# First batch of a four-stage residual kernel: w2 sent by ScalarE and subj_w by SyncE, every tile of x added on TensorE, the adapter's first product in two column tiles with the odd tiles' relu on VectorE, empty matmuls fed from a 128x128 tile

## What is computed

```python
    x = x + _L0_cond_ref(x, itok_B_0_8, L0_cond_W1, L0_cond_b1, L0_cond_W2, L0_cond_b2, L0_cond_gamma, L0_cond_beta)
    x = x + _L1_cond_ref(x, itok_B_0_7, L1_cond_weight, L1_cond_bias)
    x = x + _L2_cond_ref(x, itok_B_0_2, L2_cond_expert_wi, ...)
    x = x + _L3_cond_ref(x, L3_cond_W1, L3_cond_b1, L3_cond_v, itok_B_0_2)
```

## Time and profile before

| | us |
|---|---|
| median of 3 runs | 497.57 (497.13 to 498.37) |
| the profiled execution's own time | 497.3 |
| its span (first to last instruction) | 495.5 |
| PE busy in the span | 488.9 |

### The profile page before, as it was taken

One profiled execution on the slowest core, in us unless ns is written; L12 is line 12 of the kernel. 1 busy time (PEld: TensorE's weight loads), 2 busy tenths in 40 slices (PEclk: granted clock), 3 DMA queues, 4 the chain that ended last, 5 costly groups with the idle time before them and its releaser, 6 DMA issues.

```text
span 495.5 us, 6989 instructions
## 1 busy us (share of the span) xinstructions
PE 488.9 (99%) x2296; PEld 404.8 (82%) x2296; DVE 368.7 (74%) x750; ACT 260.6 (53%) x506; POOL 239.4 (48%) x201
## 2 busy tenths in 40 slices
PE   8999999999999999999999999999999999999996
PEld 5788888888888888888888888888888888888985
DVE  5688237997687799989578689899678779644477
ACT  4655555544457574535346666444455757445243
POOL 1575446456254446454644437444635444746023
PEclk9999999999999999999999999999999999999999
DMA  5965354322255442422237454422222342340002
GB/s 159 186 188 148 101 144 148 105 87 85 87 124 147 117 113 86 128 86 86 85 89 186 108 177 112 127 87 85 86 85 86 103 110 85 100 135 22 1 1 85
DMA packets 77657, 52.97 MB, mean 107 GB/s; under 512 B 40758, under 2 KB 67382, under 8 KB 77622
## 3 DMA queue, kind: packets, MB, share of 16 engines
q1 hardware_dynamic: 75734, 50.44, 36.2%
q10 hardware_dynamic: 1888, 2.10, 1.4%
HBM read 48.33 MB, written 2.10 MB: 102 GB/s over the span
## 4 chain that ended last, share of the span: by engine, by line
PE 96%; DVE 2%; issue 0%; ACT 0%; POOL 0%; DVEq 0%
PE ps_hid L830 15%; PE ps_hid L835 15%; PE ps_hid L831 15%; PE ps_net L892 14%; PE ps_net L887 14%; PE ps_net L888 14%; PE ps_net L859 2%; PE ps_side L538 1%; PE ps_side L542 1%; PE ps_side L537 1%; PE ps_side L548 1%; PE ps_side L551 1%; PE ps_hid L686 1%; PE ps_net L665 1%; PE ps_hid L637 0%; PE ps_hid L777 0%
## 5 line engine op out<-in xcount | busy, mean ns | idle before, releaser
L1928 POOL TENSOR_TENSOR wi_lo<-raw_wi,wi_hi 128x512 fp32r<-128x512 f32 x77 | 103.3, 1342 | 208.6 <-ACT wo_hi L1077 111.4
L1098 ACT ACTIVATE hid_hi<-ps_hid 128x512 fp32r<-128x512 f32 x160 | 95.7, 599 | 188.9 <-PE ps_hid L835 187.0
L1831 DVE SCALAR_TENSOR_TENSOR hid_lo<-ps_hid,hid_hi 128x512 fp32r<-128x512 f32 x160 | 109.6, 688 | 91.1 <-ACT hid_hi L1098 89.4
L830 PE MATMUL ps_hid<-x2T_hi,wi_lo 128*128 128x512 f32 (+1 forms) x332 | 125.3, 379 | 0.0
L831 PE MATMUL ps_hid<-x2T_hi,wi_hi 128*128 128x512 f32 (+1 forms) x332 | 125.1, 379 | 0.0
L887 PE MATMUL ps_net<-hid_hi,wo_hi 128*128 128x512 f32 x304 | 118.7, 391 | 0.0
L888 PE MATMUL ps_net<-hid_hi,wo_lo 128*128 128x512 f32 x304 | 118.5, 390 | 0.0
L1929 POOL TENSOR_TENSOR wo_lo<-raw_wo,wo_hi 128x512 fp32r<-128x512 f32 x77 | 105.6, 1371 | 0.0
L835 PE MATMUL ps_hid<-x2T_lo,wi_hi 128*128 128x512 f32 (+1 forms) x332 | 98.9, 379 | 0.0
L892 PE MATMUL ps_net<-hid_lo,wo_hi 128*128 128x512 f32 x304 | 93.9, 390 | 0.0
L831 PEld LDWEIGHTS ps_hid<-x2T_hi,wi_hi 128*128 128x128 f32 x332 | 62.4, 188 | 12.0
(11 more groups left out here) (328 smaller groups left out, 509.5 us busy)
## 6 DMA issues: line engine op xcount, KB each, us to landing
raw_wi<-in_L_cond_share_wi_dram SPq DMA_DIRECT2D x23, 512.0 KB, 3.8
raw_wo<-in_L_cond_share_wo_dram SPq DMA_DIRECT2D x23, 512.0 KB, 4.8
raw_wi<-in_L_cond_expert_wi_dram SPq DMA_DIRECT2D x16, 512.0 KB, 3.8
raw_wo<-in_L_cond_expert_wo_dram SPq DMA_DIRECT2D x16, 512.0 KB, 4.8
next_x2T<-in_x_dram SPq DMA_DIRECT2D x24, 64.0 KB, 4.3
x_rows<-in_x_dram SPq DMA_DIRECT2D x3, 512.0 KB, 4.1
x_rows<-netT SPq DMA_DIRECT2D x48, 32.0 KB, 2.0
out_dram<-out_rows SPq DMA_DIRECT2D x5, 256.0 KB, 5.7
```

The costliest lines, as they stand in the source:

```text
L830: mm(dst, wi_lo[:, w, k, c], x2T_hi[:, k, rows], start=(k == 0), stop=False)
L1098: fn(hid_hi[:, ring(b, q)], ps_hid[:, ring(b, q)], ACT.Relu).then_inc(hid_hi_ready, 1)
L1831: v.scalar_tensor_tensor(out=hid_lo[:, ring(b, q)], in0=ps_hid[:, ring(b, q)], scalar=0.0, in1=f32(hid_hi[:, ring(b, q)]), op0=ALU.max, op ...
L1928: g.tensor_tensor(wi_lo[:, w], raw_wi[:, half % 2, :, c], f32(wi_hi[:, w]), ALU.subtract)
```

## The change

In the first batch alone:

- ScalarE reads the language id instead of the subject id and issues w2 right after it, ahead of its first copy. SyncE no longer issues w2 there; it issues `subj_w`, after it has read the subject id and ahead of `subj_b`. ScalarE's `raw_wi` and `raw_wo` come right behind its first relu.
- The identity adds x for all 4 tiles (`add_x`); VectorE's sums of the odd tiles are gone, its statistics and normalisation read the banks.
- The hidden product of a half goes to one bank, tile 2h in partitions 0 to 63 and tile 2h+1 in partitions 64 to 127: 4 matmuls of 128 columns instead of 2 of 256. ScalarE takes the relu of the even tile, VectorE (`hidden_up`, with a copy of b1 in partitions 64 to 127) that of the odd one. PE's order is written out by hand.
- `zeros` is a tile of its own, 128x128 bf16, cleared first; the empty matmuls stream it four times over (still 512 columns). `edge_diag` is cleared fourth.
- `var_eps` is computed ahead of `neg_mean`, with a step of its own for each.

```diff
-        b1 = sb("b1", [A, 1])
+        b1 = sb("b1", [P, 1])
...
-        zeros = edge_diag[:, 0:S // 2].bitcast(BF16)
+        zeros = sb("zeros", [P, P], BF16)
...
+        def hidden_bank(h):
+
+            return (ps_hid[:, 2], ps_net[:, 2])[h][:, 0:P]
+
...
-                    sp.dma_start(w2[:], L0_W2[la].rearrange("o a d -> (o a) d")).then_inc(w2_in, 16)
+                    if not (isinstance(i, int) and i == 0):
+                        sp.dma_start(w2[:], L0_W2[la].rearrange("o a d -> (o a) d")).then_inc(w2_in, 16)
...
-                if not (isinstance(i, int) and i == 0):
+                if isinstance(i, int) and i == 0:
+                    sp.dma_start(subj_w[:], L1_weight[su].rearrange("o (k p) d -> p (o k) d", p=P)).then_inc(subj_in, 16)
+                else:
                     load_blocks(subj_blocks, L1_weight[su], subj_in)
...
-                for h in range(2):
-                    adapter_hidden(h)
-                    for r in (2 * h, 2 * h + 1):
-                        adapted_rows(r)
+                add_x(0)
+                adapter_hidden(0)
+                add_x(1)
+                adapted_rows(0)
+                adapted_rows(1)
+                adapter_hidden(1)
+                add_x(2)
+                add_x(3)
+                adapted_rows(2)
+                adapted_rows(3)
                 pe.wait_ge(subj_in, 16)
...
                 for k in range(KD):
-                    last = mm(ps_hid[0:A, h, 0:HS], w1[:, k], x1T[:, k, rows_half(h)], start=(k == 0), stop=(k == KD - 1))
+                    for n in range(2):
+                        last = mm(hidden_bank(h)[n * A:(n + 1) * A], w1[:, k], x1T[:, k, tile_cols(2 * h + n)], start=(k == 0), stop=(k == KD - 1), skip_group_check=True)
...
+            def add_x(r):
+
+                mm(adapted_bank(r), ident[:], x_rows[:, r], start=True, stop=False)
+
             def adapted_rows(r):

-                if r % 2 == 0:
-                    if r == 2:
-                        pe.wait_ge(p_act.sem, p_act.at(0, "hid0"))
-                    mm(adapted_bank(r), ident[:], x_rows[:, r], start=True, stop=False)
+                if r % 2:
+                    pe.wait_ge(p_dve.sem, p_dve.at(0, f"hid{r}"))
+                else:
                     pe.wait_ge(p_act.sem, p_act.at(0, f"hid{r // 2}"))
...
-                mm(adapted_bank(r), hT[:, tile_cols(r)], w2b[:], start=(r % 2 == 1), stop=True).then_inc(p_pe.sem, 1)
+                mm(adapted_bank(r), hT[:, tile_cols(r)], w2b[:], start=False, stop=True).then_inc(p_pe.sem, 1)
...
-                    mm(bank, zeros[:, 0:P], zeros[:], start=True, stop=True)
+                    mm(bank.rearrange("p (o c) -> p o c", c=P), zeros[:], zeros[:].rearrange("p (o c) -> p o c", o=1).to_broadcast([P, R, P]), start=True, stop=True)
...
-            subj = act.value_load(subj_id.rearrange("(o b) -> o b", o=1)[0:1, 0:1], min_val=0, max_val=L1_weight.shape[0] - 1)
+            lang = act.value_load(lang_id.rearrange("(o b) -> o b", o=1)[0:1, 0:1], min_val=0, max_val=L0_W1.shape[0] - 1)
+            act.dma_start(w2[:], L0_W2[bass.ds(lang, 1)].rearrange("o a d -> (o a) d")).then_inc(w2_in, 16)
...
-                fn(hT[0:A, rows_half(h)], ps_hid[0:A, h, 0:HS], ACT.Relu, bias=b1[:]).then_inc(p_act.sem, 1)
+                fn(hT[0:A, tile_cols(2 * h)], hidden_bank(h)[0:A], ACT.Relu, bias=b1[0:A]).then_inc(p_act.sem, 1)
...
             adapter_hidden(0)
-            act.dma_start(subj_w[:], L1_weight[bass.ds(subj, 1)].rearrange("o (k p) d -> p (o k) d", p=P)).then_inc(subj_in, 16)
...
+                def hidden_up(h):
+                    dve.wait_ge(p_pe.sem, p_pe.at(0, f"hid{h}"))
+                    done(v.tensor_scalar(hT[0:A, tile_cols(2 * h + 1)], hidden_bank(h)[A:P], b1[A:P], 0.0, ALU.add, ALU.max))
+
                 def statistics(r):
                     dve.wait_ge(p_pe.sem, p_pe.at(0, f"adapt{r}"))
-                    rows = adapted_bank(r)
-                    if r % 2:
-                        done(v.tensor_tensor(norm[:, r], adapted_bank(r), x_rows[:, r], ALU.add))
-                        here(f"sum{r}")
-                        rows = norm[:, r]
-                    done(v.bn_stats(stats[:, r], rows))
+                    done(v.bn_stats(stats[:, r], adapted_bank(r)))
...
+                dve.wait_ge(b1_in, 16)
+                done(v.tensor_copy(b1[A:P], b1[0:A]))
+                here("b1_up")
+                hidden_up(0)
                 statistics(0)
                 statistics(1)
                 variance(0)
+                hidden_up(1)
                 statistics(2)
                 normalise(0)
                 statistics(3)
```

22 lines of the change are left out of this document (12 added, 10 removed).

## The result

| | kernel before | changed kernel |
|---|---|---|
| median (range, runs), us | 497.49 (497.09 to 499.03, 22) | 498.15 (497.67 to 500.15, 22) |
| the profiled execution, us | 497.3 | 498.09 |
| its span, us | 495.5 | 496.1 |

The ratio of the changed kernel to the kernel before is 1.0017, with a 95% interval of 1.0009 to 1.0024: 0.7 us slower by the medians, 0.4 to 1.2 by the interval. That is a real difference, but inside the 0.3% that the forecast called no change. The forecast was 498.2 with 497.0 to 499.8.

What follows compares the result with a forecast made beforehand. PE bounds the kernel, and the change acts only in the first batch's prologue. Late `subj_w` (+0.9) less the recovered `x2T_lo` wait (0.2) gives +0.7 us on 497.3 or 497.57: forecast 498.2, eight in ten 497.0 to 499.8.

Steps and rivals of the forecast that it cites:

- The term that decides: First batch's prologue: `subj_w` sent by SyncE lands at 12.3, so the transposes of half 1 start 0.9 us later.
- behind 1 MB: `subj_w`, issued on SyncE at 8.5, has ScalarE's `raw_wi` and `raw_wo` ahead of it; landing between 11.3 and 13.1.
- The 3.3 us from the landing to the transposes of half 1: Work on PE and DVE between the landing of `subj_w` and those transposes: 12.3 + 3.3 = 15.6, against 14.72.
- The first addition falls into the wait for the copy of x: PE ahead of the hidden products: two more identity products, 0.86 us, the first within that wait, the second within the relu's.
- Column tiles: PE's hidden products: nothing saved, or half of 1.7 us; the sum took nothing, with PE at `subj_w` at 10.8 to 11.1.
- DVE: Adapter of half 1: tile 3's sum (0.42) leaves the chain; normalisation ready at about 13.9 in place of 14.58.
- w2 and zeros: Prologue start: w2 leaves at about 3.9, worth 0; empty matmuls start up to 0.25 earlier, worth 0 to 0.2.
- The recovered wait for `x2T_lo`: PE's small wait ahead of 18.41 goes, because ACT finishes the weights before the subject product: 0.2 us gained.
- The queues share: Rival, 0.22: both queues' packets take turns, `subj_w` lands at 11.3 to 11.8; change worth -0.3 to +0.2, 497.5.
- The front's gains: Rival, 0.09: `subj_w` is there when PE is, at or before 11; up to 1.0 us gained, 496.7.
- The clock in the pause: Rival, 0.15: TensorE's clock falls while PE waits for `subj_w`, adding 1.7 on top of the 0.7: 499.9.

Runs made afterwards that it cites:

- pool_raw_early: pool_subj with ScalarE sending `raw_wi` and `raw_wo` earlier, behind its two copies of x; 497.95 us, ratio 1.0007 to the kernel before.
- swap_only: The kernel before with only the transfers of the change (w2 from ScalarE, `subj_w` from SyncE behind the subject id); 498.18 us, ratio 1.0012.
- raw_later: The changed kernel with `raw_wi` and `raw_wo` written behind ScalarE's first `xbT`; 499.94 us, ratio 1.0035 to the kernel before.
- stall_filled: The changed kernel with 4 more empty matmuls ahead of TensorE's wait for `subj_w`; 498.39 us, ratio 1.0013 to the kernel before.
- front_only: The changed kernel with its transfers put back as before (`subj_w` from ScalarE, w2 from SyncE); 497.79 us, ratio 1.0002 to the kernel before.
- pool_subj: The changed kernel with GpSimd reading the subject id and sending `subj_w`; 496.94 us, ratio 0.9979 to the kernel before.
- tiles_in_turn: front_only with the hidden product's loops swapped, one column tile's matmuls after the other's; 498.19 us, ratio 1.0014 to the kernel before.
- pool_subj_again: pool_subj run once more, unchanged, beside pool_only; 496.85 us, ratio 0.9980 to the kernel before.
- pool_only: swap_only with GpSimd reading the subject id and sending `subj_w`, so the front of before; 496.99 us, ratio 0.9982 to the kernel before.
- pool_subj_late: pool_subj with GpSimd waiting until w1 has landed before it issues `subj_w`; 497.31 us, ratio 0.9985 to the kernel before.

## Why the prediction was right, and where its steps were not

**The term that decides came out right, and that was in part luck: its errors cancel.** `subj_w` landed at 12.15 (said: 12.3), PE's pause was 1.1 from the last issue at 11.07 (said: 1.2), half 1's transposes came at 15.42 (said: 15.6). But it was issued at 7.86, not 8.5: from the end of gamma's issue (5.85) it took 2.0 us and not 2.5, 1.8 of them the read of the id, which ran for the most part before the burst; in pool_raw_early, inside the burst, the read took 3.8. That should have made it early. Against it ACT's burst began at 7.41, not 6.9. And "behind 1 MB" was not so in this execution: with its issue ended at 8.23 and that of `raw_wo` at 8.31, `subj_w` was served ahead of `raw_wo`, which landed at 13.57. What stood in front of it was `raw_wi` alone and that transfer's slow beginning (0.04 MB from 8 to 9 us, 0.30 from 9 to 10). swap_only, raw_later and stall_filled, where ACT is earlier, have the case that the prediction described, with landings at 12.73, 12.99 and 12.75. (The sum itself, redone with its own terms, gives 12.2 rather than 12.3: 6.9 + 1.0 + 3.5 + 0.3 + 0.5.) The 3.3 us from the landing to the transposes of half 1 held: 12.15 to 15.42.

**"The first addition falls into the wait for the copy of x": wrong.** The identity product, two instructions of 0.43 each or more, starts at 5.48, just when the copy is ready (4.87 + 0.60), and the hidden products start at 6.47 against 5.60. In the kernel before the spacing of the transposes of x went from 0.213 to 0.110 at 4.9 us; here it was 0.213 through the last of them, at 5.26, and the same in front_only and pool_subj. The columns came at half speed. That this is the clock at its lower level is inferred from the spacing: the view by stretches shows a granted clock of 1.00 from the start on. It fits that the record of the granted clock kept in the trace, which no view prints, begins only at 6.81 here and at 4.90 in the kernel before. Where the spacing changed early (tiles_in_turn, pool_subj_again: by 4.1) the additions did fall into the shade, and hidden started at 5.20 and 5.46. pool_only is the old front in a run of the slow kind (0.213 through 5.48): it lost 0.23 there, 5.83 against 5.60, where the new one started 0.9 late. So the new front gains or loses with the clock's first rise, and that differs between executions of one and the same kernel (last section).

**Column tiles: the sum took the wrong bound.** They run side by side, 0.39 for 8 instructions. PE still arrived late: the last `w2b` product starts at 11.07, where the sum had PE at `subj_w` at 10.8 to 11.1, since the saving only paid for the late start. As the prediction said, the sum did not hang on it.

**DVE: partly.** The sum of tile 3 is gone, but the normalisation of half 1 was ready at 14.53, not 13.9 (14.57 before): DVE's last small operations ended at the same time as before (12.96, 12.92), because PE's products came 0.2 later, and ACT had the copy of `subj_w` to do until 13.93. It stayed in the shade of the wait, as said.

**w2 and zeros: as said, within 0.1.** w2 left at 4.06 and the copies still start at 4.87 (4.95); PE's empty matmuls began at 0.98 (1.32), and the transposes of x at 3.74 (3.85).

**The recovered wait for `x2T_lo`: mostly not recovered.** +0.70 at the transposes of half 1 became +0.51 at 18.92 (18.41 before), but +0.66 at the first product of 512 columns (21.57, 20.91): a later product waited for `x2T_lo` at 20.5. So the sum's +0.9 and -0.2 came out as +0.70 and -0.04, and its total of 0.7 owes something to that too.

**The rivals.** The queues share: refuted for these two queues. The front's gains: they do not come through even where `subj_w` is on time (front_only; pool_subj_again against pool_only), for a reason that no rival had: the weights behind it, and SP's row of small transfers, are the next limit. The clock in the pause: by the counts it occurred in about a quarter of the runs, 6 of 22, at +2.0 (said: +1.7). For the median it was a miss; as a mechanism it is likely, not seen.

**What stays open.** In the profiled runs only part of the 0.8 us between pool_only and the kernel before is seen: the stretch from the first product of 512 columns to the last matmul is 469.72 against 469.96 (the kernel before has two starts 0.32 and 0.34 apart at 39.3, pool_only none), with the pair of weights landed at 12.50 against 13.09 and the next issue at 12.51 against 13.48. That before loses more there in runs with an early clock is likely and was not shown.

## What to carry over

Before moving a transfer between SyncE's queue and ScalarE's, list every issue of both by the time at which it ends, and put the transfer into that list: in these runs what mattered was who was ahead there, not whose queue it was. (For GpSimd's queue the runs don't show such a rule: in pool_subj w2's packets moved beside those of `subj_w`.) Send what is needed first from a queue that can issue it first, and count the id that it must read before. A shorter stage in front gains only until the next landing that it doesn't move; look for that landing in the trace (here the next 1 MB, at 22) before optimising the stage. And take more than one profile before believing a figure from the first microseconds.

## What the runs showed of the hardware beyond what was expected

- The moment of the first rise of TensorE's clock differs between executions, with the work before it alike. Two profiled runs of one and the same kernel: in pool_subj the transposes of x stood 0.213 apart to their end and the run took 497.74; in pool_subj_again they went to 0.109 from 4.0 on and it took 496.39. The hidden products started at 6.54 and 5.46. The 1.35 us between these two runs is more than the transfers (0.8) or the new front (0.14) were worth, so a single profile can't judge such an edit.
- The same 256 KB by GpSimd's queue took 3.4 to 3.7 us from the start of the issue (4.32 to 8.02 in pool_subj), of which GpSimd itself is busy for 0.97; in pool_subj_late 3.3 (5.79 to 9.12). That is slower than the 2.65 on SP's queue with nothing ahead, and faster than any of the cases with a burst ahead.
- Reading an id into a register took 1.8 us on SP in the quiet and 3.8 (6.59 to 10.35, tiles_in_turn) while ACT's burst moved.
